# Four hand-written instruction orders of a two-layer decoder kernel, rearranged

## What is computed

```
x = LN(x + attention(x))             # 16 heads of 16, causal softmax, biases
x = LN(x + long_conv(ctx, ctx, x))   # see below, kernel ssm_kernel, skip D
x = LN(x + ternary_ffn(x))           # 256 -> 1024 (silu gate * up) -> 256
x = LN(x + state_space(x))           # conv of 4 taps, chunked scan, 8 heads, gated norm
x = LN(x + long_conv(x, ctx, ctx))   # kernel k, skip fside
x = LN(x + hadamard_ffn(x))          # quantised inputs, ternary weights, Hadamard ahead of down

# long_conv(k, v, q): 16 groups of 8 rows of length 256
kv  = k[i] * v[j]                    # every pair of rows of a group
y   = causal_convolution(kv, kernel of the group) + kv * skip
out = sum over i of y[i, j] * q[i]
```

## Time and profile before

| | us |
|---|---|
| runs | 749.12, 746.75, 749.25 |
| median | 749.12 |
| profiled execution | 746.65 |
| its span in the trace | 744.0 |
| busy: PE, DVE, POOL, ACT | 696.2, 610.1, 538.3, 412.4 |

### The profile page before, as it was taken

One profiled execution on the slowest core, in us unless ns is written; L12 is line 12 of the kernel. 1 busy time (PEld: TensorE's weight loads), 2 busy tenths in 40 slices (PEclk: granted clock), 3 DMA queues, 4 the chain that ended last, 5 costly groups with the idle time before them and its releaser, 6 DMA issues. The chain is left out here.

```text
span 744.0 us, 13795 instructions
## 1 busy us (share of the span) xinstructions
PE 696.2 (94%) x4302; PEld 497.2 (67%) x4302; DVE 610.1 (82%) x1281; ACT 412.4 (55%) x660; POOL 538.3 (72%) x781
## 2 busy tenths in 40 slices
PE   6999999999989999999889989989999999999994
PEld 5788888754434677778667777755544457777783
DVE  4887888688979978665799899878999998877873
ACT  0665757710160744554598877872010348889784
POOL 2788798878857425530248668789898999999972
PEclk9999999999999999999999999999999999999997
DMA  8910000000300050000031121204000000000001
GB/s 282 365 52 2 2 2 3 1 1 0 141 29 1 0 217 1 1 2 1 29 103 72 44 71 34 80 1 131 1 0 1 0 2 1 15 16 15 9 22 44
DMA packets 12727, 33.39 MB, mean 45 GB/s; under 512 B 2672, under 2 KB 8048, under 8 KB 11376
## 3 DMA queue, kind: packets, MB, share of 16 engines
q1 hardware_dynamic: 12656, 32.52, 12.1%
HBM read 30.35 MB, written 2.16 MB: 44 GB/s over the span
## 5 line engine op out<-in xcount | busy, mean ns | idle before, releaser
L1053 PE MATMUL bank<-XT,win_late 128*128 128x256 f32 x320 | 81.3, 388 | 5.9 <-ACT ss_sz L1151 2.8
L564 POOL TENSOR_TENSOR m_kv<-CTXT 128x512 f32<-128x512 f32 x64 | 65.2, 1043 | 16.9 <-PE bank L596 16.9
L619 DVE TENSOR_REDUCE MIX<-m_pr 128x128 f32<-128x1024 f32 x64 | 77.0, 1210 | 0.3
L1238 DVE SCALAR_TENSOR_TENSOR ss_xc<-bank,cw_late,ss_xc 128x254 f32<-128x254 f32 x144 | 67.4, 477 | 4.9 <-ACT ss_xc L1142 1.4
L564 POOL TENSOR_TENSOR m_kv<-XT,CTXT 128x512 f32<-128x512 f32 x64 | 69.4, 1111 | 1.4 <-PE bank L596 1.1
L1053 PEld LDWEIGHTS bank<-XT,win_late 128*128 128x128 f32 x320 | 56.6, 190 | 17.6 <-DVE ss_xc L1238 5.6
L594 PE MATMUL bank<-m_kv,toep 128*128 128x512 f32 x128 | 66.1, 598 | 1.2 <-issue 1.2
L596 PE MATMUL bank<-m_kv,toep 128*128 128x512 f32 x128 | 66.3, 599 | 0.0
L595 PE MATMUL bank<-m_kv,toep 128*128 128x512 f32 x128 | 66.0, 597 | 0.0
L1530 PE MATMUL bank<-had_last,f_ht 128*128 128x256 f32 x256 | 60.2, 382 | 0.1
L750 PE MATMUL bank<-wd,f_pmt 128*128 128x256 f32 x256 | 59.7, 380 | 0.0
(11 more groups left out here) (247 smaller groups left out, 1884.8 us busy)
## 6 DMA issues: line engine op xcount, KB each, us to landing
MIX<-cum_rows SPq DMA_DIRECT2D x15, 512.0 KB, 3.4
toep<-toep_dram SPq DMA_DIRECT2D x2, 2048.0 KB, 12.4
X<-x_dram SPq DMA_DIRECT2D x1, 2048.0 KB, 12.5
CTXT<-ctxT_dram SPq DMA_DIRECT2D x1, 2048.0 KB, 17.6
out_dram<-f_o SPq DMA_DIRECT2D x16, 128.0 KB, 1.7
XT<-xT_dram SPq DMA_DIRECT2D x1, 1280.0 KB, 8.2
win_late<-win_dram SPq DMA_DIRECT2D x1, 1280.0 KB, 5.2
wgu<-wgu_dram SPq DMA_DIRECT2D x1, 1024.0 KB, 5.0
```

The lines of the kernel that those rows point to most:

```text
L564: m = nc.gpsimd.tensor_tensor(KV[n % 3][:, c, :, :].rearrange("p (b j) i -> p b j i", b=HB), ki, vj, ALU.mult)
L619: nc.vector.tensor_reduce(head(MIX)[:, :, a, bass.ts(h, HB), :], PR[n % 2][:, :, :, :].rearrange("p c (b j) i -> p c b j i", b=HB), op=ALU ...
L1053: m = nc.tensor.matmul(bX[(NU * g + n) % 3][:, 0:GS_], win[:, h, off:off + P], XT[:, h, bass.ts(g, GS_)], start=(h == 0), stop=(h == C - 1))
L1238: m = nc.vector.scalar_tensor_tensor(acc[:, :, sh:S], bank[:, :, 0:S - sh], cw[:, r, n:n + 1], acc[:, :, sh:S], ALU.mult, ALU.add)
```

## The change

The four lists are replaced by other orders of the same calls. Of 886 calls on PE 674 stand at another place, of 632 on ACT 477, of 1066 on DVE 872, of 479 on POOL 368; the farthest moves are 14 places on PE, 15 on ACT, 26 on DVE and 30 on POOL. Operations, tiles, semaphores, waits and SP's order are the same. A line or two of each list:

```diff
 def tensor_order(a, m, f, x, n, g):
...
-    m.mix(9); m.mix(10); m.mix(11); a.x_turn(12); m.mix(12); m.mix(13); a.x_turn(13); m.mix(14); a.x_turn(14); m.mix(15); m.mix(16); a.x_turn(15)
-    m.mix(17); m.mix(18); m.mix(19); m.mix(20); m.mix(21); m.totals(); m.mix(22); f.mix_turn(0); m.mix(23); m.mix(24); f.mix_turn(1); m.mix(25)
...
+    m.mix(9); a.x_turn(12); m.mix(10); a.project(15); m.mix(11); a.x_turn(13); m.mix(12); a.x_turn(14); m.mix(13); a.x_turn(15); m.mix(14); m.mix(15)
+    m.mix(16); m.mix(17); m.mix(18); m.mix(19); m.mix(20); m.totals(); m.mix(21); f.mix_turn(0); m.mix(22); m.mix(23); f.mix_turn(1); m.mix(24)
...
 def scalar_order(a, m, f, x, n, g):
...
-    m.magnitude(0); m.magnitude(1); m.magnitude(2); m.to_whole(0); m.to_whole(1); m.ternary(0); f.keep_q(0); m.ternary(1); f.silu(0, 1); f.silu(0, 0)
...
+    a.keep_x(15); m.magnitude(0); m.magnitude(1); m.magnitude(2); m.sign0(2); m.to_whole(0); m.to_whole(1); m.ternary(0); f.keep_q(0); f.silu(0, 1)
...
 def vector_order(a, m, f, x, n, g):
...
-    x.taps(0, 5); x.dt_copy(); x.dt_first(); x.dt_rest(); x.keep_sums(); x.taps(1, 0); x.taps(1, 1); x.first_args(); x.taps(1, 2); x.taps(1, 3)
...
+    x.dt_first(); x.dt_rest(); x.taps(1, 0); x.keep_sums(); x.taps(1, 1); x.taps(1, 2); x.first_args(); x.taps(1, 3); x.taps(1, 4); x.mask(0)
...
 def gpsimd_order(a, m, f, x, n, g):
...
-    m.mix(12); m.mix(13); a.diagonal(7); a.rstd(14); m.mix(14); m.mix(15); m.mix(16); a.rstd(15); m.mix(17); m.mix(18); m.consts(); m.mix(19)
...
+    a.residual(15); m.mix(11); m.mix(12); a.diagonal(7); a.rstd(14); m.mix(13); a.rstd(15); m.mix(14); m.mix(15); m.consts(); m.mix(16); m.mix(17)
```

More of the change, by code:

```diff
@@ L1883, in tensor_order @@
-    f.down(14, 0); f.p_turn(15, 1); f.x_turn(11); x.unit(0, 0); f.down(14, 1); x.unit(0, 1); f.p_turn(15, 0); f.x_turn(12); x.unit(0, 2)
-    f.down(15, 0); f.down(15, 1); x.unit(0, 3); f.x_turn(13); x.unit(0, 4); f.x_turn(14); x.unit(0, 5); f.x_turn(15); x.dt_product(); x.dt_turn()
-    x.unit(0, 6); x.unit(0, 7); x.unit(0, 8); x.unit(0, 9); x.unit(1, 0); x.x_back(0); x.unit(1, 1); x.unit(1, 2); x.sums(); x.first_rows()
-    x.c_times_b(0); x.x_back(1); x.unit(1, 3); x.unit(1, 4); x.unit(1, 5); x.unit(1, 6); x.unit(1, 7); x.c_times_b(1); x.scan(0); x.unit(1, 8)
@@ L1899, in tensor_order @@
-    x.scan(12); x.square_sum(10); x.unit(7, 7); x.out_product(10); x.square_sum(11); x.unit(7, 8); x.x_turn(6, 12); x.c_times_b(14); x.x_turn(7, 12)
-    x.x_back(14); x.x_back(15); x.unit(7, 9); x.c_times_b(15); x.x_turn(8, 12); x.x_turn(9, 12); x.scan(13); x.out_product(11); n.mix(0); n.mix(1)
-    x.scan(14); x.out_product(12); x.scan(15); x.x_turn(10, 12); n.mix(2); x.square_sum(12, 11); n.mix(3); n.mix(4); x.square_sum(13, 11); n.mix(5)
-    n.mix(6); x.out_product(13); x.square_sum(14, 11); n.mix(7); x.x_turn(11, 15); x.out_product(14); n.mix(8); x.out_product(15)
@@ new lines, in tensor_order @@
+    f.down(14, 0); f.p_turn(15, 0); f.p_turn(15, 1); f.x_turn(11); f.down(14, 1); x.unit(0, 1); x.unit(0, 2); f.down(15, 0); f.x_turn(12)
+    f.down(15, 1); x.unit(0, 3); f.x_turn(13); x.unit(0, 4); f.x_turn(14); x.unit(0, 5); f.x_turn(15); x.dt_product(); x.dt_turn(); x.unit(0, 6)
+    x.unit(0, 7); x.unit(0, 8); x.unit(0, 9); x.unit(1, 0); x.unit(1, 1); x.x_back(0); x.unit(1, 2); x.sums(); x.x_back(1); x.unit(1, 3)
+    x.first_rows(); x.unit(1, 4); x.c_times_b(0); x.unit(1, 5); x.unit(1, 6); x.unit(1, 7); x.scan(0); x.unit(1, 8); x.c_times_b(1); x.unit(1, 9)
@@ new lines, in tensor_order @@
+    x.out_product(10); x.unit(7, 7); x.square_sum(11); x.x_back(14); x.x_turn(6, 12); x.x_turn(7, 12); x.unit(7, 8); x.c_times_b(14); x.scan(13)
+    x.x_back(15); x.unit(7, 9); x.c_times_b(15); x.out_product(11); x.x_turn(8, 12); n.mix(0); x.scan(14); x.out_product(12); x.x_turn(9, 12)
+    n.mix(1); x.scan(15); n.mix(2); x.x_turn(10, 12); n.mix(3); x.square_sum(12, 11); n.mix(4); n.mix(5); x.square_sum(13, 11); x.out_product(13)
+    n.mix(6); n.mix(7); x.square_sum(14, 11); x.out_product(14); x.x_turn(11, 15); n.mix(8); x.square_sum(15, 12); x.out_product(15); n.mix(9)
```

596 lines of the change are left out of this document (297 added, 299 removed).

## The result

The changed kernel took 719.69 us in the median (719.3 to 720.58, 4 runs), the kernel before 747.93 us beside it (745.67 to 749.25, 4 runs). The ratio is 0.9627, 95% interval 0.9598 to 0.9656: faster by 28 us. That is outside the forecast range of 730 to 750, and almost four times the 7.4 us that the prediction took off.

The account below looks back on a forecast made before the run. TensorE (PE) was taken to bound the kernel, so only its 47.8 us idle could move. Gains of 9.4 us less 2.0 for new waits gave 7.4 off the 749.1 median: 741.7 us, range 730 to 750.

Parts of the forecast that it names:

- Six places: Totals, quantised block, sign, step sizes, scan of block 7, down products: gains 5.0 + 0 + 0.65 + 1.0 + 1.0 + 1.7, 9.4 us.
- more than I count: Rival: the new order also takes half of the other 22 us of PE's middle idle time, 730.7 us; chance 0.16.
- The totals: m.totals, weight sums of the last FFN in the first mixer: wait 3.52 and slow clock behind it go, 5.0 us.
- DVE's limit: First mixer: DVE rests 2.39 and 2.66 us because of the totals stall, so can give up 5.05 us, no more.
- The quantised block: f.q_turn(0) and last multiply: PE waits 0.94 and 1.62 us for full DVE; credited 0, other bound 2.6.
- The sign: m.sign0(1) on ACT, ahead of the copy PE needs in attention: moved later, PE's 1.00 us wait goes, 1.0.
- The scan of block 7: State space: PE waits 2.03 us for DVE's late, long x.matrix; earlier decay counted half, 1.0, bounds 0 and 2.0.
- The step sizes: x.keep_sums, state space start: PE's 0.65 us wait for two copies goes, 0.65; lower bound 0 if taps are late.
- The down products: g.down(2) and g.down(3), last FFN: waits of 0.72 and 1.00 us covered by more PE work ahead, 1.7.
- The charge of 2.0 for new waits: Scans 0 and 1, state space: c_times_b comes about 2.5 us closer; two waits, between 0 and 4.1, charged 2.0.
- The slow rival: State space: DVE and POOL collisions cost 1.45 us each; 12 more blocks hit give 759 us; chance 0.13.

Follow-up runs that it names:

- 1.2 alone: Kernel before with four priced terms moved together (sign, decay, step sizes, both down products), one or two calls each: 748.87 us against 747.23, ratio 1.0026.
- the halves: Kernel before with the new order only in the first half of the state space: 742.59 us, ratio 0.9939; the second half was not run.
- the first stretch alone: Kernel before with the new order only in attention up to x_turn(12), mixer steps 0 to 11: 742.32 us against 747.22, ratio 0.9935.
- the second stretch alone: Kernel before with the new order only from mixer step 12 to the end of the first FFN: 740.54 us, ratio 0.9913.
- the fourth stretch alone: Kernel before with the new order only from step 14 of the second mixer to the end: 743.13 us, ratio 0.9957.
- the totals alone: Kernel before with totals two mixer steps later on PE, scales two later on DVE, first turn and add behind: 742.73 us against 747.23, ratio 0.9939.
- the third stretch alone: Kernel before with the new order only from the state space's step sizes to step 13 of the second mixer: 734.28 us, ratio 0.9826.
- the two runs that test theory D: Kernel before with the four terms' moves, without down(3)'s move: 744.82 us against 747.56; or with DVE's add_down(3) moved too: 745.87 us, ratio 0.9983.

## Why the prediction was wrong

- **What bounds the kernel** was right: PE's work is the same, and all that the change moved is PE's waiting. But the page understates the waiting: between the first matmul and the last it shows 34.8 us, and the distances of starts give 63.7.
- **The step that failed is the choice of terms**: "I cost the places where PE waits and the new order puts more work ahead of the waiting instruction", and then "Elsewhere the leads of DVE and ACT over PE go both ways by a microsecond or two and I cost them at nothing". Six places were priced, most of them with long waits. The 105 waits of 0.1 to 1 us, 33.0 us in all, were not, but for two, and they gave 14.9 of the 25.7 us. By places, the priced and charged ones gave 11.8 us, and those costed at nothing 14. In the state space the prediction counted 1.65 us of gain and 2.0 of loss; the stretch gave 13.0 us. Of its 24.8 us of lost time only 2.03 and 0.65 were priced.
- **The rival "more than I count"** was the right one in kind. It took half of the other waits and came to 730.7 us. By distances its terms leave 52 us of other waits, of which half is 26 and the time 716, an estimate. That half is not worked out from anything; of all the lost time 40% went.
- **The totals** were right: 5.0 us forecast, 4.6 measured alone, no wait left, clock at 1.00. **DVE's limit** of 5.05 us held at that place: by distances the totals and the step behind them lost 5.2 us before, and nothing after the change. **The quantised block** was credited at 0, which was too low. Its waits lost 3.2 us by distance before and 1.8 after, so 1.4 were gained. In the same stretch two DVE operations beside POOL's products are back at their usual length, 1.5 us of DVE's time (below); that this is what made room was not tested alone.
- **The sign** was right: 1.0 forecast, 1.2 alone. **The scan of block 7** came out near its number, 1.0 forecast and 0.9 alone, but by luck. The prediction said that the earlier decay "moves the start, not the 2.67". In the run the long form left the matrix, the whole wait of 2.03 went, and half of it came back behind the next DVE operation.
- **The step sizes**: 0.65 forecast, 0.2 alone; a wait of PE for the taps followed, near the lower bound. **The down products**: 1.7 forecast; alone the first gave 0.5 at most and the second lost 3.7. The prediction priced a move on PE's list and did not ask what stands behind its consumer in DVE's list.
- **The charge of 2.0 for new waits** was half right: the wait at scan 0 came with 0.84 us, the one at scan 1 did not.
- **The slow rival** (collisions) did not come. On DVE's own lines of the state space the summed time stayed within 1 us: the matrices lost 2.8 us of excess, the gated multiplies gained 2.3.

What stays open is which of the many moves in the state space gives how much; the halves gave 4.6 and, by difference, 8.4 us. So the failed step is shown, but the cause is followed only to half a stage, not to single waits.

## What to carry to other kernels

When the orders of all engines are replaced together, do not forecast from the few long waits: add up every short one on the engine that sets the time, by the distances of its starts rather than by its idle time, and give the sum as the upper end; here 40% of it was gained. When a single call is moved by hand, look first at where its consumer stands in the other engines' lists and what is behind it there; a move that takes one wait away on PE lost 3.7 us, and still 1.6 when DVE's list followed but not ACT's. Cuts at which all lists have the same calls ahead let each stretch be tried alone, and here their gains added within the spread of the runs.

## What the runs showed of the hardware

Two DVE operations ahead of the last steps of the first mixer were three times as long in the kernel before, while POOL made the next products. Before, POOL and DVE:

```profile
233.73 2.08 POOL L564 TENSOR_TENSOR m_kv<-CTXT 128x512 f32<-128x512 f32 x2
233.76 1.16 DVE L848 TENSOR_SCALAR f_z<-X,f_sc 128x256 f32<-128x256 f32 x1
234.84 1.12 DVE L469 TENSOR_SCALAR X<-f_y,f_mv,f_rs 128x256 f32<-128x256 f32 x1
```

Changed:

```profile
221.96 0.34 DVE L848 TENSOR_SCALAR f_z<-X,f_sc 128x256 f32<-128x256 f32 x1
...
224.54 0.40 DVE L469 TENSOR_SCALAR X<-f_y,f_mv,f_rs 128x256 f32<-128x256 f32 x1
```

Together that is 1.16 + 1.12 - 0.34 - 0.40 = 1.5 us of DVE's time. The Trainium skill ("SBUF — State Buffer", section "Who interferes with whom") names `tensor_scalar` among the operations that can take the port pair which DVE shares with GpSimd, when their operands meet its conditions, and says that whichever issues first blocks the other for its whole length; the trace agrees, POOL having started 0.03 us earlier. The same section says that on trn2 `tensor_reduce` never contends; the trace agrees, as the 64 sums of the mixers (L619) take 1.16 to 1.22 us in both kernels, whatever POOL does.

TensorE's clock made the same wait cost more in one execution than in another. Five traces have the wait of 2.03 us ahead of the scan of block 7, with the same calls around it. With the first and with the second stretch alone the granted clock is 0.50 behind it, that is 1.2 GHz, and 1.7 us more are lost there. With the fourth stretch alone, with the totals alone and in the kernel before it stays at 1.00. The windows behind the scan, with the first stretch alone and then before, columns as in the earlier trace rows:

```profile
434.50:437.80 3.30, 3.30 (x10) 2.67 (x9) 3.19 (x9) 1.19 (x3) 1.93 (x2) 0.50 0.21 58
```

```profile
438.50:441.80 3.30, 3.30 (x18) 2.92 (x18) 3.19 (x9) 2.17 (x4) 2.83 (x3) 1.00 0.18 66
```

Ahead of the totals eight traces have the wait of some 3.5 us, and all of them the clock of 0.50 behind it. The step behind lost 1.5 to 1.8 us in five of them, and 2.7 with the third stretch alone and in the two runs that test theory D. The 1.48 us of the prediction was one of these values. A change that takes such a wait away can therefore gain more in the median than one trace shows.
